# Attention and expert kernel: the last group's second residual sum ahead of the next batch's second low weights

## The chip, the cores and the metric

The kernel runs on one core of a Trainium2 chip. The core has five engines with an instruction queue each: TensorE (matmul), VectorE, ScalarE, GpSimd and SyncE, the last issuing most DMA transfers. They run side by side and wait for each other by semaphores that the kernel names itself. The metric is the device time of one execution in microseconds (us), the median of several runs.

## The reference

Four sequences of 2048 tokens, 256 features each, pass a causal attention without softmax (signs of the inputs as queries and keys, a sigmoid as weights), a residual sum and a layer norm, and then a layer of 32 experts with one expert per token, a residual sum and a second layer norm. Cut to what matters:

```python
Q = ste_sign(x * bq); K = ste_sign(x * bk); V = x * bv     # bq, bk, bv: signs of the biases
scores = jnp.einsum('btd,bsd->bts', Q, K) * scale
attn = jnp.where(causal, jax.nn.sigmoid(scores * 4.0), 0.0)
x = _layernorm(x + jnp.einsum('bts,bsd->btd', attn, V))
# experts: logits = xt @ w_router; top-1 expert, at most C tokens each
y = jnp.einsum('ecf,efh->ech', jax.nn.silu(g) * u, w_down)
x = _layernorm(x + out_tok * gate)
```

## The kernel before

**Tiling.** The attention takes up the first 300 us or so. Each batch (sequence) is cut into four groups of 512 queries. Group g meets 4g + 4 key tiles of 128, one per step, which gives NS = 40 steps per batch: steps 0 to 3 for group 0, 4 to 11 for group 1, 12 to 23 for group 2 and 24 to 39 for group 3. In the last four steps of a group the key tile lies on the diagonal and the step has 512, 384, 256 and 128 query columns. Group 0 has diagonal steps alone.

**A step on the engines.** TensorE computes the scores of a step into one of SB = 4 PSUM banks (line 910, four steps ahead). ScalarE takes the sigmoid twice: into the high weights, rounded (line 703), and back into PSUM in full (line 705). VectorE subtracts the two, which gives the low weights (`low`, line 1202). TensorE then multiplies high and low weights with high and low values (`values`, lines 932 to 934, three matmuls for each of the step's tiles of 128 queries) and adds up over the steps of the group in two PSUM banks, two tiles of 256 columns in each. The scores of step k + 4 wait for the low weights of step k, whose bank they overwrite.

**The end of a group.** When the first two of the group's four tiles are complete, VectorE adds the input to them (`residual`, line 1209, one 128x512 sum for one bank), and later does the same for the other two. The semaphore `pv_done` counts finished value steps: the first sum of a group waits for the group's last step but two, the second for the last step. The next group's first step overwrites both banks; TensorE's first matmul into each waits for the sum that reads it (`res_ready`). The row statistics follow (lines 1216 and 1224), and GpSimd, ScalarE, TensorE and VectorE turn them into the normalised rows, the router's logits and the places in the experts' buffers, spread over the steps of the next group by tables at the top of the file.

**What sets the order.** Each engine's order is written out by the program: `batch` on VectorE runs over the 40 steps, puts `low(b, k)` first in each, and then whatever the tables place at step k. `SUM[g]` holds the steps of the two sums of group g, `ROWS[g]` that of the first two tiles' statistics, `STATS[g]` that of the others and of the aggregation. A step of 40 or more means step k - 40 of the next batch. So `SUM[3] = (40, 41)` puts the first sum of group 3 behind `low` of the next batch's step 0 and the second behind that of its step 1. After the last batch the two sums are written out separately and don't read the table.

```python
                    for g in range(NG):
                        for i in (0, 2):
                            if k == SUM[g][i // 2]:
                                add_pair(b, g, i)
                            if k + NS == SUM[g][i // 2] and not first:
                                add_pair(b - 1, g, i)
                        if k == ROWS[g]:
                            row_statistics(b * NG + g, 0, g % 2)
                        if k + NS == ROWS[g] and not first:
                            row_statistics((b - 1) * NG + g, 0, g % 2)
```

**The experts.** From about 310 us on, TensorE runs gate, up and down projections expert by expert; the order there is a separate program.

Of the kernel before, what the change touches and what calls it, by code (L numbers as in the profile page):

```python
# [38 lines left out]

SUM = {0: (4, 4), 1: (13, 13), 2: (23, 24), 3: (40, 41)}
ROWS = {0: 5, 1: 13, 2: 24, 3: 41}
STATS = {3: 1, 0: 6, 1: 17, 2: 25}
NORM = {3: (6, 6, 7, 7), 0: (10, 11, 11, 11), 1: (21, 22, 23, 23), 2: (30, 31, 31, 32)}
# [18 lines left out]
def bass_postln_attn_moe_kernel(nc, x, bv_q, bv_k, bv_v, w_router, w_gate, w_up, w_down, out):  # L64
# [25 lines left out]
    with ExitStack() as ctx:  # L90
# [1069 lines left out]
        def _(dve):  # L1160
# [150 lines left out]
            def add_pair(b, g, i):  # L1311
                residual(b * NG + g, i, b * NS + END[g] - GT + i + 2, g % 2)

            def batch(b, first, last):
                for k in range(NS):
# [9 lines left out]
# [6 lines that stand above are left out]
# [200 lines left out]
```

How the kernel before makes its waits and increments, by code:

```python
        def atleast(eng, s, value, settle=False):  # L265
            if isinstance(value, int) and value <= 0:
                return
            if settle and not isinstance(value, int):
                value = eng.to_reg(value)
                eng.wait_ge(consts, 11)
            eng.wait_ge(s, value)
# [49 lines left out]
        @block.sync  # L324
# [5 lines left out]
            for h, landed in enumerate((x_half, x_in[0])):
                src = x[0, h * GQ // 2:(h + 1) * GQ // 2, :].rearrange("(i p) d -> p i d", p=P)
                sp.dma_start(xall[:, h * GT // 2:(h + 1) * GT // 2, :], src).then_inc(landed, 16)
            sp.dma_start(bv_row[:, :], bv_v.partition_broadcast(P)).then_inc(bv_row_in, 16)
            load_x(0, 1)
            sp.dma_start(w_r[:, :, :], w_router.rearrange("(c p) e -> p c e", p=P)).then_inc(w_r_in, 16)
            for q in range(2, NG):
                load_x(0, q)
            sp.wait_ge(zero_step, 3)
            zrows = buf_rows.rearrange("(n p r) w -> n p (r w)", p=P, r=ZR)
            for n in range(SLOTS // (P * ZR)):
                sp.dma_start(zrows[n], zero).then_inc(zero_out, 16)
# [6 lines left out]
            def turn_signs(b, q):  # L350
                sp.wait_ge(sgn_ready, b * NG + q + 1)
                sp.wait_ge(scores_ready, (b - 1) * NS + min(NS, OFF[3] + GT * q + GT))
                sp.dma_start(q_t[:, q, :, :].rearrange("p c (i t) -> p (c i) t", t=P),
                             sgn[:, :, :, :].rearrange("p c i d -> p (c i d)"), transpose=True).then_inc(qt_in, 16)
```

## Time and profile before

| | us |
|---|---|
| median of 3 runs | 536.95 |
| lowest, highest | 536.78, 537.89 |
| the profiled execution | 540.78 |
| its span, first to last instruction | 539.1 |
| TensorE matmuls busy | 516.2 (96%) |
| TensorE weight loads busy | 457.1 (85%) |
| VectorE busy | 407.4 (76%) |
| ScalarE busy | 378.9 (70%) |
| GpSimd busy | 377.6 (70%) |

A profile is one execution; the row times below belong to it and not to the median. PE is TensorE (PEld its weight loads), DVE VectorE, ACT ScalarE, POOL GpSimd. Matmuls overlap in the records, since they are pipelined and their ends are modelled: how fast TensorE goes is read from start to start. A timeline row has the start, the duration, the engine, the line, the operation, the output and inputs, their shapes and, in brackets, how long the engine was idle ahead of it and who released it.

### The profile page before, as it was taken

To read this page: it belongs to the slowest core of one execution; us is meant where nothing else is said; L and a number is where in the kernel's file an instruction comes from. 1 tells how busy PE (TensorE), PEld (TensorE's weight loads), DVE (VectorE), ACT (ScalarE), POOL (GpSimd) and SP (SyncE) were. 2 spreads that over 40 slices of the span, in tenths; PEclk is the share of its full clock that TensorE was granted. 3 is DMA by queue.
4 is the path that set the end of the run, shared out by engine and by line. 5 is a ranking of instruction groups with operands and counts; after the bars stand their busy time and mean duration, and the time that the engine had idled before them with its cause. 6 is when DMAs were issued, how large, how long until landed. Compare 5 with 4: busy or idle time off the path is not lost.

```text
span 539.1 us, 12188 instructions
## 1 busy us (share of the span) xinstructions
PE 516.2 (96%) x4021; PEld 457.1 (85%) x4021; DVE 407.4 (76%) x1031; ACT 378.9 (70%) x774; POOL 377.6 (70%) x497
## 2 busy tenths in 40 slices
PE   6999999999999999999999988999999999999992
PEld 5889898898888898988989747999988999999981
DVE  4884877876878948688766636888888888888873
ACT  5886968868878879688786513677767667777752
POOL 4647867776879688777775270577777777787776
PEclk9999999999999999999999999999999999999997
DMA  7995332263332433338741016477586666776211
GB/s 253 374 356 181 87 99 61 79 177 101 109 84 80 124 108 79 91 49 274 229 171 62 2 44 157 125 232 216 179 257 195 198 198 208 220 234 191 76 41 51
DMA packets 91919, 81.54 MB, mean 151 GB/s; under 512 B 31642, under 2 KB 83082, under 8 KB 91856
## 3 DMA queue, kind: packets, MB, share of 16 engines
q1 hardware_dynamic: 84320, 66.38, 41.7%
q0 software_dynamic: 6912, 14.30, 7.7%
q8 instruction: 33, 0.54, 0.4%
q14 instruction: 30, 0.25, 0.2%
q10 hardware_dynamic: 624, 0.07, 0.1%
HBM read 44.33 MB, written 37.90 MB: 153 GB/s over the span
## 4 chain that ended last, share of the span: by engine, by line
PE 86%; DVE 3%; issue 3%; POOL 3%; DMA 2%; ACT 1%; SPq 0%; ACTq 0%; DVEq 0%; POOLq 0%
PE ps L932 11%; PE ps L934 11%; PE ps L933 11%; PE ps L910 10%; PE ps L1096 8%; PE ps L1104 7%; PE ps L1097 7%; PE ps L1122 5%; PE ps L1130 3%; PE ps L1069 3%; PE ps L951 2%; PE ps L964 2%; PE ps L1119 1%; PE ps L1121 1%; PE ps L1120 1%
## 5 line engine op out<-in xcount | busy, mean ns | idle before, releaser
L932 PE MATMUL ps<-v_hl,hl_ring 128*128 128x256 f32 x544 | 178.2, 328 | 1.6 <-DVE xs L1209 1.4
L933 PE MATMUL ps<-v_hl,hl_ring 128*128 128x256 f32 x544 | 153.3, 282 | 0.0
L934 PE MATMUL ps<-v_hl,hl_ring 128*128 128x256 f32 x544 | 153.1, 281 | 0.0
L932 PEld LDWEIGHTS ps<-v_hl,hl_ring 128*128 128x128 f32 x544 | 103.3, 190 | 17.6 <-DVE xs L1209 2.1
L1202 DVE TENSOR_TENSOR hl_ring<-ps,hl_ring 128x512 fp32r<-128x512 f32 (+3 forms) x160 | 94.1, 602 | 21.3 <-ACT ps L705 14.9
L933 PEld LDWEIGHTS ps<-v_hl,hl_ring 128*128 128x128 f32 x544 | 103.4, 190 | 2.7
L703 ACT ACTIVATE hl_ring<-ps 128x512 fp32r<-128x512 f32 (+3 forms) x160 | 86.2, 539 | 24.3 <-PE ps L910 24.0
L934 PEld LDWEIGHTS ps<-v_hl,hl_ring 128*128 128x128 f32 x544 | 103.1, 190 | 0.0
L705 ACT ACTIVATE ps<-ps 128x512 f32<-128x512 f32 (+3 forms) x160 | 87.4, 547 | 0.0
L910 PE MATMUL ps<-q_t,k_t 128*128 128x512 bf16 (+3 forms) x320 | 85.0, 349 | 0.2 <-DVE hl_ring L1202 0.2
L542 POOL DMA_INDIRECT expert_rows<-xrow,slot x64 | 64.4, 1007 | 29.4 <-issue 23.2
L1096 PE MATMUL ps<-hl_ring,v_hl 128*128 128x320 f32 x256 | 80.8, 328 | 0.3 <-DVE hl_ring L1473 0.3
L1097 PE MATMUL ps<-hl_ring,v_hl 128*128 128x320 f32 x256 | 76.0, 309 | 0.0
L626 POOL DMA_INDIRECT out_dram<-alone,ids x55 | 61.5, 1118 | 19.5 <-issue 17.4
L826 ACT ACTIVATE a_buf<-ps 128x320 f32<-128x320 f32 x64 | 27.9, 437 | 43.1 <-PE ps L1104 24.2
L1096 PEld LDWEIGHTS ps<-hl_ring,v_hl 128*128 128x128 f32 x256 | 48.1, 188 | 7.0 <-issue 6.5
L1308 DVE TENSOR_TENSOR v_hl<-xall,v_hl 128x1280 fp32r<-128x1280 f32 x32 | 47.9, 1498 | 7.1 <-issue 7.1
L1097 PEld LDWEIGHTS ps<-hl_ring,v_hl 128*128 128x128 f32 x256 | 48.1, 188 | 0.4
L1104 PE MATMUL ps<-hl_ring,v_hl 128*128 128x320 f32 x256 | 47.9, 309 | 0.0
L495 POOL TENSOR_TENSOR v_hl<-z,v_hl 128x1024 fp32r<-128x1024 f32 x15 | 36.0, 2398 | 12.0 <-ACT v_hl L695 12.0
L741 ACT ACTIVATE v_hl<-xall 128x1280 fp32r<-128x1280 f32 x32 | 40.5, 1264 | 0.2 <-PE ps L934 0.2
L1104 PEld LDWEIGHTS ps<-hl_ring,v_hl 128*128 128x128 f32 x256 | 40.2, 188 | 0.0
(170 smaller groups left out, 1104.4 us busy)
## 6 DMA issues: line engine op xcount, KB each, us to landing
expert_rows<-xs SPq DMA_DIRECT2D x40, 258.0 KB, 5.8
xs<-expert_rows SPq DMA_DIRECT2D x32, 258.0 KB, 2.8
out_dram<-alone SPq DMA_DIRECT2D x16, 512.0 KB
xall<-in_L_ffn_w_gate_dram SPq DMA_DIRECT2D x32, 256.0 KB
xall<-in_L_ffn_w_up_dram SPq DMA_DIRECT2D x32, 256.0 KB
xall<-in_L_ffn_w_down_dram SPq DMA_DIRECT2D x32, 256.0 KB
xall<-in_L_attn_x_dram SPq DMA_DIRECT2D x15, 512.0 KB, 5.6
xs<-expert_rows SPq DMA_DIRECT2D x31, 64.5 KB, 3.4
```

Of the source, the lines that this page charges most:

```text
L542: g_.indirect_dma_start(out=buf_rows, out_offset=bass.IndirectOffsetOnAxis(ap=slot[:, par, i:i + 1], axis=0), in_=xrow[:, par, i, :], in_o ...
L626: g_.indirect_dma_start(out=out_rows, out_offset=bass.IndirectOffsetOnAxis(ap=ids[:, e % NIDS, t:t + 1], axis=0), in_=o_s[e % 3][:, t, :], ...
L703: s_.activation(hl_ring[:, 0, k % WRING, lo:GQ], ps[:, k % SB, lo:GQ], ACT.Sigmoid, scale=0.25)\
L705: s_.activation(ps[:, k % SB, lo:GQ], ps[:, k % SB, lo:GQ], ACT.Sigmoid, scale=0.25)\
L910: last = mm(o, k_t[:, c, j * P:(j + 1) * P], q_t[:, g, c, lo:GQ], start=(c == 0 and not diag), stop=(c == DC - 1), skip_group_check=diag)
L932: mm(o, ah, v_hl[:, 0, j, :], start=(j == 0 and i % 2 == 0), stop=False, skip_group_check=True)
L933: mm(o, ah, v_hl[:, 1, j, :], start=False, stop=False, skip_group_check=True)
L934: last = mm(o, al, v_hl[:, 0, j, :], start=False, stop=(j == GT * g + i), skip_group_check=True)
L1096: mm(o, wh, xh[:, c, :], start=(c == 0), stop=False)
L1097: mm(o, wl, xh[:, c, :], start=False, stop=False)
L1104: last = mm(o, wh, xl[:, c, :], start=False, stop=(c == DC - 1))
L1202: v_.tensor_tensor(hl_ring[:, 1, r, lo:GQ], ps[:, k % SB, lo:GQ], hl_ring[:, 0, r, lo:GQ].bitcast(F32), ALU.subtract).then_inc(al_ready, 1)
```

## The change

One number of a table: the second residual sum of group 3 is placed at step 40, with the first, instead of step 41.

```diff
-SUM = {0: (4, 4), 1: (13, 13), 2: (23, 24), 3: (40, 41)}
+SUM = {0: (4, 4), 1: (13, 13), 2: (23, 24), 3: (40, 40)}
 ROWS = {0: 5, 1: 13, 2: 24, 3: 41}
 STATS = {3: 1, 0: 6, 1: 17, 2: 25}
```

The rows below are VectorE's at the first change of batch; the same stands at the second and third. Row 1202 with 512 columns is `low` of the new batch's step 0, with 384 that of step 1, with 256 and 128 those of steps 2 and 3; rows 1209 are the two sums of the old batch's group 3 (the tile `xs` is the second of the two buffers for sums), and 1191 are keys. Before:

```order
L1202 TENSOR_TENSOR hl_ring<-ps,hl_ring 128x512 [waits pv_done,a_ready,ah_ready]
L1209 TENSOR_TENSOR xs<-ps,xall 128x512 [waits x1_ready,pv_done]
L1202 TENSOR_TENSOR hl_ring<-ps,hl_ring 128x384 [waits pv_done,a_ready,ah_ready]
L1209 TENSOR_TENSOR xs<-ps,xall 128x512 [waits x1_ready,pv_done]
L1216 BN_STATS stats<-xs 128x6 [waits res_ready]
L1216 BN_STATS stats<-xs 128x6
L1216 BN_STATS stats<-xs 128x6 [waits res_ready]
L1216 BN_STATS stats<-xs 128x6
L1224 BN_AGGR mv<-stats 128x2 [waits rstd_step,stats_step]
L1224 BN_AGGR mv<-stats 128x2 x3
L1191 TENSOR_SCALAR k_t<-q_t,qk_sgn 128x512 [waits qt_in]
L1202 TENSOR_TENSOR hl_ring<-ps,hl_ring 128x256 [waits pv_done,a_ready,ah_ready]
```

And with the change:

```order
L1202 TENSOR_TENSOR hl_ring<-ps,hl_ring 128x512 [waits pv_done,a_ready,ah_ready]
L1209 TENSOR_TENSOR xs<-ps,xall 128x512 [waits x1_ready,pv_done] x2
L1202 TENSOR_TENSOR hl_ring<-ps,hl_ring 128x384 [waits pv_done,a_ready,ah_ready]
L1216 BN_STATS stats<-xs 128x6 [waits res_ready]
L1216 BN_STATS stats<-xs 128x6
```

The second sum has changed places with step 1's low weights; the statistics, the keys and all later rows keep their order.

On TensorE nothing moves. The piece of its order at the same place shows who waits for these rows: step 0's value matmuls (12 of them, in two halves of six), and the scores of step 5 behind them.

```order
L932 MATMUL ps<-v_hl,hl_ring 128x256 [waits al_ready,res_ready,ah_ready,v_ready]
L933 MATMUL ps<-v_hl,hl_ring 128x256
L934 MATMUL ps<-v_hl,hl_ring 128x256
L932 MATMUL ps<-v_hl,hl_ring 128x256
L933 MATMUL ps<-v_hl,hl_ring 128x256
L934 MATMUL ps<-v_hl,hl_ring 128x256
L932 MATMUL ps<-v_hl,hl_ring 128x256 [waits res_ready]
L933 MATMUL ps<-v_hl,hl_ring 128x256
L934 MATMUL ps<-v_hl,hl_ring 128x256
L932 MATMUL ps<-v_hl,hl_ring 128x256
L933 MATMUL ps<-v_hl,hl_ring 128x256
L934 MATMUL ps<-v_hl,hl_ring 128x256
```

This is the same before and with the change: the first `res_ready` is the first sum's, the second the second's, and the next row, the scores of step 5, waits for `al_ready`, which low weights of step 1 post.

## Rows read from the trace of the kernel before

**Rows 1.** The page: TensorE's busy time, and the chain that ended last, by engine
```profile
PE 516.2 (96%) x4021; PEld 457.1 (85%) x4021; DVE 407.4 (76%) x1031; ACT 378.9 (70%) x774; POOL 377.6 (70%) x497
...
PE 86%; DVE 3%; issue 3%; POOL 3%; DMA 2%; ACT 1%; SPq 0%; ACTq 0%; DVEq 0%; POOLq 0%
```

**Rows 2.** Who waited for whom, TensorE, 0 to 305 us: total us, times, longest us
```profile
PE ps L932 <- DVE xs L1209: 1.4, 3, 0.6
```

**Rows 3.** Timeline of TensorE at the first change of batch
```profile
83.16 0.28 PE L934 MATMUL ps<-v_hl,hl_ring 128*128 128x256 f32 x1
...
83.94 0.36 PE L932 MATMUL ps<-v_hl,hl_ring 128*128 128x256 f32 x1
...
84.61 0.28 PE L934 MATMUL ps<-v_hl,hl_ring 128*128 128x256 f32 x1
...
85.44 0.39 PE L932 MATMUL ps<-v_hl,hl_ring 128*128 128x256 f32 x1 [0.56 <-DVE xs L1209]
...
86.26 0.61 PE L910 MATMUL ps<-q_t,k_t 128*128 128x512 bf16 x2
...
87.78 0.60 PE L910 MATMUL ps<-q_t,k_t 128*128 128x512 bf16 x2
```

**Rows 4.** Timeline of VectorE at the same place
```profile
83.11 0.68 DVE L1209 TENSOR_TENSOR xs<-ps,xall 128x512 f32<-128x512 f32 x1
84.23 0.56 DVE L1202 TENSOR_TENSOR hl_ring<-ps,hl_ring 128x384 fp32r<-128x384 f32 x1 [0.44 <-issue]
84.70 0.68 DVE L1209 TENSOR_TENSOR xs<-ps,xall 128x512 f32<-128x512 f32 x1
85.30 1.40 DVE L1216 BATCH_NORM_STATS2 stats<-xs 128x6 f32<-128x256 f32 x4
...
87.27 0.62 DVE L1202 TENSOR_TENSOR hl_ring<-ps,hl_ring 128x256 fp32r<-128x256 f32 x2
```

**Rows 5.** Timeline of ScalarE there: the second sigmoid of step 1
```profile
83.65 0.49 ACT L705 ACTIVATE ps<-ps 128x384 f32<-128x384 f32 x1
```

**Rows 6.** Timeline, end of group 0: its last matmul, and the sum behind it
```profile
89.61 0.28 PE L934 MATMUL ps<-v_hl,hl_ring 128*128 128x256 f32 x1
...
89.98 0.69 DVE L1209 TENSOR_TENSOR res<-ps,xall 128x512 f32<-128x512 f32 x1 [0.64 <-issue]
```

**Rows 7.** Timelines of TensorE and VectorE at the third change of batch
```profile
230.60 0.28 PE L934 MATMUL ps<-v_hl,hl_ring 128*128 128x256 f32 x1
...
231.68 0.56 DVE L1202 TENSOR_TENSOR hl_ring<-ps,hl_ring 128x384 fp32r<-128x384 f32 x1 [0.44 <-ACT hl_ring L703]
...
232.06 0.28 PE L934 MATMUL ps<-v_hl,hl_ring 128*128 128x256 f32 x1
...
232.89 0.39 PE L932 MATMUL ps<-v_hl,hl_ring 128*128 128x256 f32 x1 [0.55 <-DVE xs L1209]
```

**Rows 8.** Timelines of VectorE and TensorE at the second change of batch
```profile
157.36 0.56 DVE L1202 TENSOR_TENSOR hl_ring<-ps,hl_ring 128x384 fp32r<-128x384 f32 x1 [0.44 <-ACT hl_ring L703]
158.30 0.69 DVE L1209 TENSOR_TENSOR xs<-ps,xall 128x512 f32<-128x512 f32 x1 [0.39 <-PE ps L934]
158.91 1.40 DVE L1216 BATCH_NORM_STATS2 stats<-xs 128x6 f32<-128x256 f32 x4
...
160.87 0.62 DVE L1202 TENSOR_TENSOR hl_ring<-ps,hl_ring 128x256 fp32r<-128x256 f32 x2
...
157.28 0.28 PE L934 MATMUL ps<-v_hl,hl_ring 128*128 128x256 f32 x1
...
158.44 0.28 PE L934 MATMUL ps<-v_hl,hl_ring 128*128 128x256 f32 x1
...
159.05 0.39 PE L932 MATMUL ps<-v_hl,hl_ring 128*128 128x256 f32 x1 [0.33 <-DVE xs L1209]
...
161.38 0.61 PE L910 MATMUL ps<-q_t,k_t 128*128 128x512 bf16 x2
```

**Rows 9.** Timeline of ScalarE behind the first change of batch: step 5's first sigmoid
```profile
87.29 0.60 ACT L703 ACTIVATE hl_ring<-ps 128x512 fp32r<-128x512 f32 x1 [1.21 <-PE ps L910]
```

## The prediction

> **What bounds the kernel now.** I read the busy shares and the chain of waits first. TensorE's matmuls are busy 96% of the span and carry 86% of the chain that ended last [rows 1]. So an edit on VectorE changes the time only where TensorE waits for it. The view of who waited for whom, cut to the attention (0 to 305 us), names one such wait on the moved line: TensorE stood three times for the residual sums of line 1209, 1.4 us in all, 0.6 us the longest [rows 2]. Three is the number of batch boundaries, and the changed table entry acts at those alone; the last batch ends in code of its own. I then read the timeline at each boundary.
>
> I call the two halves of step 0's value matmuls pair 1 and pair 2 (six matmuls each). Pair 1 needs the first residual sum, pair 2 the second, since each overwrites the PSUM bank that the sum reads. "Low n" is VectorE's line 1202 of step n of the new batch, and "step 39" the last step of the old one.
>
> At the first boundary, pair 1 runs from 83.94 to 84.61, five spacings in 0.67 us, so 0.13 us apart. The next matmul, which opens pair 2, starts only at 85.44 [rows 3]. Of these 0.83 us, 0.70 us is a hole. VectorE shows why: its first sum starts at 83.11, then it is idle 0.44 us ahead of low 1 (84.23), then the second sum starts at 84.70 and takes 0.68 us, to 85.38. Pair 2 follows 0.06 us behind that end [rows 4]. Low 1 waited for ScalarE's second sigmoid of step 1, 83.65 plus 0.49 = 84.14 [rows 5]. So the second sum waits, by its place in the queue, for a ScalarE result that it does not use. Its own input was there: the last matmul of step 39 starts at 83.16 [rows 3], and elsewhere a sum starts 0.37 us behind such a start (89.61 to 89.98) [rows 6], which would be 83.53 here.
>
> The third boundary has the same shape: 232.06 to 232.89, again a hole of 0.70 us, with step 39's last matmul at 230.60 and low 1 at 231.68 [rows 7]. The second boundary differs. Low 1 starts at 157.36, and the second sum at 158.30, behind 0.39 us of idle put down to TensorE; that is 1.02 us behind the start of step 39's last matmul (157.28). The hole is 158.44 to 159.05, so 0.61 - 0.13 = 0.48 us [rows 8].
>
> **The change, part by part.** Nothing is added or removed: in each of three boundaries one 128x512 sum (0.68 us) goes ahead of one 128x384 low weights (0.56 us). The steps are the same on TensorE, ScalarE, GpSimd and SyncE, and no DMA moves.
>
> First boundary. From the start of a sum to that of the next instruction 0.60 us pass (84.70 to 85.30), from low 1 to the next 0.47 us (84.23 to 84.70) [rows 4]. The second sum then starts at 83.11 + 0.60 = 83.71, which is behind the 83.53 above, and ends at 84.39. Pair 2 is due at 84.61 + 0.13 = 84.74 and no longer waits: 0.70 us gained there. Low 1 starts at 83.71 + 0.60 = 84.31, 0.08 us later than now, and ends at 84.87. Who needs it? The scores of step 5, now at 86.26, then at 85.56 [rows 3]: covered by 0.7 us. What is late next is low 2. The row statistics start at 84.31 + 0.47 = 84.78 instead of 85.30, so everything behind them on VectorE is 0.52 us earlier, and low 2 starts at 86.75 instead of 87.27. The scores of step 6 need it. They start 0.51 us behind low 2's start at all three boundaries (87.78 behind 87.27, 161.38 behind 160.87 [rows 3, 4, 8]). Their place behind the matmuls ahead of them would be 87.78 - 0.70 = 87.08; VectorE allows 86.75 + 0.51 = 87.26, or 0.06 us less if those 0.51 us hold some slack. So 0.52 to 0.58 us of the 0.70 us stay. I take **0.55 us** for the first boundary, and by the same rows **0.55 us** for the third.
>
> The spacing decides here, so a rule of the Trainium skill is weighed against it. The row shows the instruction behind the sum starting at 85.30, 0.08 us before the sum's end at 85.38 [rows 4]. The Trainium skill (VectorE: DVE Perf Modes, The DRAIN you can't avoid) says that the next operation does not start until the pipeline is empty. By a strict end-to-start chain the second sum would start at 83.79, low 1 at 84.47 and the statistics at 85.03, and each boundary would keep 0.27 us. The rows measure the overlap, so I go by 0.60 us.
>
> Second boundary. Here the second sum already starts when TensorE's signal comes, 158.30, and it cannot start sooner by standing earlier. If the signal is as late as in this trace, pair 2 stays at 159.05, and low 1, whose inputs were ready at 157.36, is now queued behind the waiting sum: 158.30 + 0.60 = 158.90. The statistics start at 159.37 instead of 158.91, low 2 at 161.33, the scores of step 6 at 161.78 to 161.84 instead of 161.38: a loss of 0.40 to 0.46 us. If the signal comes 0.37 us behind the matmul's start, as in rows 6, the sum runs 157.65 to 158.33, pair 2 is due at 158.57, low 1 starts at 158.25, the statistics at 158.72, low 2 at 160.68 and the scores of step 6 at 161.13 to 161.19: a gain of 0.19 to 0.25 us. I take a loss of **0.2 us**, between these ends and nearer to the one that this trace shows.
>
> Behind the boundaries I cost nothing: at the first ScalarE idles 1.21 us for the scores of step 5 before it takes up step 5 at 87.29 [rows 9], so it moves up with TensorE, and the statistics, which GpSimd waits for, come earlier by 0.52 us at two boundaries. What a boundary gives is a shift of all that follows.
>
> Sum: -0.55 - 0.55 + 0.2 = **-0.9 us**, between -0.65 (late signal at the second) and -1.4 (prompt one, top of each span). The profiled execution took 540.78 us with a span of 539.1; the median of the runs is 536.95 (536.78 to 537.89). I put the difference on the median: 536.0 us. Differences under 0.2%, about 1.07 us, are what a measurement of this kernel cannot tell from none, so the forecast lies inside that band and near its edge.
>
> **Rivals.**
>
> *All three boundaries gain (535.3 us).* If TensorE, 0.55 us earlier through the second batch, meets the second boundary as it met the others, that boundary gives 0.55 us too: -1.65 us. For: two of three show this form, and the late signal occurs once. Against: at the second boundary TensorE was not stopped ahead of pair 1, and the sum had to wait for it even behind low 1.
>
> *The gain is absorbed (about 537.0 us).* ScalarE and VectorE share later due points with TensorE in the new batch (normalising, transposes, routing), and if one of those is set by ScalarE's own work, TensorE waits there for what it gained. For: ScalarE has little idle time between steps 6 and 9. Against: the wait of 1.21 us in rows 9, which shows ScalarE behind TensorE and not ahead of it.
>
> *A new wait in front of low weights (slower, 538.3 us).* The second sum now stands between low 0 and low 1, and everything behind it waits for step 39's last matmul. In the first boundary, with the sum starting at s, low 2 starts at s + 0.60 + 0.47 + 1.97 (85.30 to 87.27) and the scores of step 6 0.51 us later; this equals 87.78 at s = 84.23, 1.07 us behind that matmul's start. Beyond that point each 0.1 us costs 0.1 us. The second boundary, at 1.02 us, already loses 0.40 to 0.46 us, since low 1 had been done early there. If the signal came 1.5 us behind the matmul at the other two, all three would lose 0.45 us, 1.35 us in all: 538.3 us. Against: no row shows 1.5 us, and the release of rows 6 is 0.37 us. The Trainium skill (Perfetto Trace Analysis, Tensor Engine Instruction) says that a matmul's reported end is computed, and that its semaphore goes out only when PSUM has acknowledged the writes. By that rule the shown ends don't bound the signal; the 1.02 us of rows 8 agree with it.
>
> That the change does something else than it says is excluded: three pairs of VectorE steps change places.
>
> **How the numbers follow.** Forecast (two gain, the second between its ends): 0.48. All three gain: 0.25. Absorbed: 0.13. New wait: 0.14. Faster by over 0.2%: all of the second case and about a quarter of the first (-1.07 to -1.4), 0.37. Slower by over 0.2%: most of the last, 0.12. The rest, 0.51, lies within. The range: below, all three gain plus the scatter of the runs (the lowest is 0.17 below the median) and some for phases that shift, 534.9; above, the absorbed case and the half of the new wait, 537.7.
>
> **What would show it.** Right: second sums at the first and third boundary start 0.6 us behind the first ones; the wait of TensorE on line 1209 falls from 1.4 to near 0.4 us or less; low 2 is 0.5 us nearer to step 39 there; a short wait appears at the scores of step 6. The idle time of VectorE at line 1209 put down to TensorE at the second boundary grows. Wrong: TensorE still waits 0.5 us ahead of pair 2, or sums that start over 1 us behind step 39's last matmul at two or more boundaries, or the gain seen at 90 us but gone before 150 us.

## The result, and the profile after

The change made the kernel slower: 538.35 us (median of 19 runs) against 537.08 us for the kernel before (19 runs beside them), a ratio of 1.0022 with a 95% interval of 1.0014 to 1.0029. That is 1.27 us, just over the 0.2% that a measurement of this kernel can tell. The forecast was 0.9 us the other way, and 538.35 lies outside its range.

The execution profiled before took 540.78 us while the kernel's runs lie at 537, so the span of the changed kernel's profile (536.4 us) must not be held against that trace's 539.1.

The page of the changed kernel, the lines that answer to [rows 1]:

```profile
PE 512.6 (96%) x3983; PEld 457.6 (85%) x4021; DVE 407.6 (76%) x1031; ACT 380.7 (71%) x774; POOL 384.7 (72%) x497
...
PE 88%; DVE 4%; issue 3%; POOL 2%; DMA 2%; ACT 0%; SPq 0%; ACTq 0%; DVEq 0%; POOLq 0%
```

The record of the changed kernel lacks 38 matmuls (3983 against 4021), so its busy time of TensorE says nothing beside [rows 1]. Who waited for whom on TensorE, 0 to 305 us (total us, times, longest):

```profile
PE ps L970 <- ACT lg_t L725: 1.2, 3, 0.4
PE ps L910 <- DVE hl_ring L1202: 1.0, 4, 0.3
```

The wait on line 1209 [rows 2] is gone, and a wait of the scores (L910) on the low weights (L1202) has come at the changes of batch. Whether the first was ever there in an ordinary execution of the kernel before is the first thing to ask.

The third change of batch in the changed kernel, VectorE and then TensorE, which answers to [rows 7]:

```profile
228.49 0.69 DVE L1209 TENSOR_TENSOR xs<-ps,xall 128x512 f32<-128x512 f32 x1
...
230.08 0.69 DVE L1209 TENSOR_TENSOR xs<-ps,xall 128x512 f32<-128x512 f32 x1 [0.90 <-PE ps L934]
...
230.69 0.55 DVE L1202 TENSOR_TENSOR hl_ring<-ps,hl_ring 128x384 fp32r<-128x384 f32 x1
...
233.11 0.62 DVE L1202 TENSOR_TENSOR hl_ring<-ps,hl_ring 128x256 fp32r<-128x256 f32 x2
...
229.70 0.28 PE L934 MATMUL ps<-v_hl,hl_ring 128*128 128x256 f32 x1
...
231.57 0.28 PE L934 MATMUL ps<-v_hl,hl_ring 128*128 128x256 f32 x1
...
233.09 0.28 PE L934 MATMUL ps<-v_hl,hl_ring 128*128 128x256 f32 x1
...
233.59 0.60 PE L910 MATMUL ps<-q_t,k_t 128*128 128x512 bf16 x2 [0.22 <-DVE hl_ring L1202]
...
234.62 0.28 PE L934 MATMUL ps<-v_hl,hl_ring 128*128 128x256 f32 x1
```

The last value matmuls (L934) of four steps stand here: step 39 of the old batch at 229.70, steps 0, 1 and 2 of the new one at 231.57, 233.09 and 234.62. VectorE starts the first sum 1.21 us *ahead* of step 39's last matmul (228.49 against 229.70). It then idles 0.90 us and starts the second sum 0.38 us behind that matmul. Low 1, low weights of step 1, stands behind it, and low 2 starts at 233.11. TensorE had no hole in step 0's values (231.57 is 1.87 us behind 229.70), but step 1's last value matmul starts at 233.09 and the scores of step 6 only at 233.59: 0.50 us where 0.12 is usual (232.16 to 232.28 in the kernel before, shown further down), so 0.38 us lost.

### The profile page after: what moved, and what is told of

Same layout as the page of the kernel before. It is cut to its first block, busy times and chain, and to the rows that moved or that the text cites. A ratio compares the mean times of both kernels' runs of the same rounds, so it can differ in the third digit from the quotient of the medians.

```text
span 536.4 us, 12150 instructions
## 1 busy us (share of the span) xinstructions
PE 512.6 (96%) x3983; PEld 457.6 (85%) x4021; DVE 407.6 (76%) x1031; ACT 380.7 (71%) x774; POOL 384.7 (72%) x497
## 4 chain that ended last, share of the span: by engine, by line
PE 88%; DVE 4%; issue 3%; POOL 2%; DMA 2%; ACT 0%; SPq 0%; ACTq 0%; DVEq 0%; POOLq 0%
PE ps L932 12%; PE ps L933 11%; PE ps L934 11%; PE ps L910 10%; PE ps L1096 8%; PE ps L1104 7%; PE ps L1097 7%; PE ps L1122 5%; PE ps L1130 3%; PE ps L1069 3%; PE ps L951 2%; PE ps L964 2%; PE ps L1119 1%; PE ps L1121 1%; PE ps L1120 1%
## 5 line engine op out<-in xcount | busy, mean ns | idle before, releaser
L934 PE MATMUL ps<-v_hl,hl_ring 128*128 128x256 f32 x544 | 153.1, 281 | 0.0
L1202 DVE TENSOR_TENSOR hl_ring<-ps,hl_ring 128x512 fp32r<-128x512 f32 (+3 forms) x160 | 93.9, 601 | 19.1 <-ACT ps L705 13.6
L934 PEld LDWEIGHTS ps<-v_hl,hl_ring 128*128 128x128 f32 x544 | 103.1, 190 | 0.0
L910 PE MATMUL ps<-q_t,k_t 128*128 128x512 bf16 (+3 forms) x286 | 77.4, 345 | 3.8 <-issue 1.3
L626 POOL DMA_INDIRECT out_dram<-alone,ids x55 | 57.0, 1035 | 16.6 <-issue 14.4
L1096 PEld LDWEIGHTS ps<-hl_ring,v_hl 128*128 128x128 f32 x256 | 48.1, 188 | 7.0 <-issue 6.5
L1097 PEld LDWEIGHTS ps<-hl_ring,v_hl 128*128 128x128 f32 x256 | 48.2, 188 | 0.4
L844 ACT ACTIVATE alone<-z,zrs 128x256 f32<-128x256 f32 x54 | 29.0, 594 | 17.6 <-POOL zrs L613 16.3
```

The lines of the kernel that those rows point to most:

```text
L626: g_.indirect_dma_start(out=out_rows, out_offset=bass.IndirectOffsetOnAxis(ap=ids[:, e % NIDS, t:t + 1], axis=0), in_=o_s[e % 3][:, t, :], ...
L910: last = mm(o, k_t[:, c, j * P:(j + 1) * P], q_t[:, g, c, lo:GQ], start=(c == 0 and not diag), stop=(c == DC - 1), skip_group_check=diag)
L934: last = mm(o, al, v_hl[:, 0, j, :], start=False, stop=(j == GT * g + i), skip_group_check=True)
L1096: mm(o, wh, xh[:, c, :], start=(c == 0), stop=False)
L1097: mm(o, wl, xh[:, c, :], start=False, stop=False)
L1202: v_.tensor_tensor(hl_ring[:, 1, r, lo:GQ], ps[:, k % SB, lo:GQ], hl_ring[:, 0, r, lo:GQ].bitcast(F32), ALU.subtract).then_inc(al_ready, 1)
```

## The experiments

Two theories went in. Theory 1: at the changes of batch VectorE is usually ahead of TensorE, so the moved sum finds its input missing and holds low weights 1 and all behind them. Theory 2: the boundaries are as in the first profile, and the time is lost later. After the first four runs, theory 1 took its later form: executions come in two kinds, and the change's sign follows from the kind. In the *late* kind (the kernel before near 540.5 us) VectorE and ScalarE start over 1 us behind the matmul that they wait for, at certain places; in the *prompt* kind (near 537 us) 0.3 to 0.4 us behind it.

### The kernel before again, in runs at 540.5 us

No edit.

> The kernel before once more, for its profile. Theory 1 (the profile read for the prediction was not the usual execution; usually VectorE is ahead of TensorE at every change of batch, so that the second sum waits for step 39 even behind the low weights of step 1): the span is about 535.4 us, and at all three changes of batch the second sum starts about 0.4 us behind step 39's last matmul, with idle time before it, and TensorE's wait on line 1209 is under 0.3 us in all. Theory 2 (the boundaries are as in the first profile, and what they give is lost later): holes of 0.7 us ahead of pair 2 at the first and third change of batch again.

The kernel before had a median of 540.54 us in these runs, 3.5 us more than beside the changed kernel, and its span was 539.0. All three changes of batch have the form of [rows 3]; TensorE's waits in the attention:

```profile
PE ps L932 <- DVE xs L1209: 1.7, 3, 0.6
```

The expected span of 535.4 us and the missing holes did not come, so by this profile alone theory 2 holds. But the time had moved too: the first profile and this one are of executions near 540.5 us, and the result is of executions near 537.

### The wait alone, low weights 1 behind step 39

```diff
-                atleast(dve, pv_done, n - WRING + 1)
+                atleast(dve, pv_done, b * NS if k == 1 else n - WRING + 1)
```

> The order of before, but low weights of step 1 of a new batch wait for the last value step of the old batch. Theory 1 (low weights 1, and all behind them, held by that wait are the cost): as slow as the change, 1.002 to 1.003, about +1.2 us, and a wait of 0.3 to 0.4 us at the scores of step 6. Theory 2 (the cost comes from where the second sum stands or from what the statistics set off later): less than half of that, 1.000 to 1.001.

1.0002 (0.9991 to 1.0013), beside the same runs of the kernel before: theory 1, as it stood then, had 1.002 to 1.003 here and missed. Where the kernel before takes 540.5 us, low weights 1 come behind that signal anyway (84.30, released by ScalarE, 1.06 us behind step 39's last matmul at 83.24), and the wait costs nothing.

### The first pair's statistics directly behind the first sum

```diff
-ROWS = {0: 5, 1: 13, 2: 24, 3: 41}
+ROWS = {0: 5, 1: 13, 2: 24, 3: 40}
```

> The order of before, but the first pair's statistics go from behind the second sum to directly behind the first sum (0.7 us of VectorE work into its idle time). Theory 1: low weights of step 2 come 0.3 to 0.7 us earlier at each change of batch; if they hold the scores of step 6 in the kernel before, 0.998 to 0.999, if they don't, 1.000. Theory 2: no change, or slower if the low weights of step 1 are held.

1.0018 (1.0007 to 1.0029), slower, where theory 1 expected 1.000 or less and theory 2 allowed for a loss. At the first change of batch the timeline shows the first sum at 83.34 and the second at 85.19, 1.85 us apart instead of 1.59 (83.11 to 84.70 in [rows 4]): in these runs low weights 1 and the second sum set TensorE's hole, and the 0.75 us of statistics don't fit into 0.44 us of idle time.

### The change at the first change of batch alone

```diff
-                            if k + NS == SUM[g][i // 2] and not first:
+                            if k + NS == (40 if g == 3 and b in BOUND else SUM[g][i // 2]) and not first:
```

with `BOUND = (1,)` and the table of before.

> The change at the first change of batch alone. Theory 1 (each change of batch costs 0.4 us): +0.4 us, 1.0005 to 1.0012. Theory 2 (a loss that grows out of one place, or a gain there): outside of that, either about 0 or the whole +1.2 us.

0.9987 (0.9974 to 1.0000): by the median a *gain* of about 0.7 us, with none at the edge of the interval. Theory 1, as it stood, had a loss. The traces are sharper than the times. From step 39's last value matmul to step 2's last, the first change of batch took 5.62 us in the kernel before of this set (the first two rows) and 5.06 us here (the last two): 0.56 us gained, as the prediction had it for such a boundary (0.55). The second and third change of batch, left as before, took 5.66 and 5.65 us here.

```profile
83.66 0.28 PE L934 MATMUL ps<-v_hl,hl_ring 128*128 128x256 f32 x1
...
89.28 0.28 PE L934 MATMUL ps<-v_hl,hl_ring 128*128 128x256 f32 x1
...
83.41 0.28 PE L934 MATMUL ps<-v_hl,hl_ring 128*128 128x256 f32 x1
...
88.47 0.28 PE L934 MATMUL ps<-v_hl,hl_ring 128*128 128x256 f32 x1
```

### The change and the kernel before again

In the next set of runs the kernel before took 537.34 us, so this is the prompt kind.

> The change as it is, beside the kernel before on one chip. Theory 1 now: executions come in two kinds. In one (kernel before near 540.5 us) TensorE's signals are late at about 19 places, VectorE is late at the changes of batch and the change gains 0.4 to 0.55 us at each, so the ratio is 0.996 to 0.998. In the other (kernel before near 537 us) the signals are prompt, VectorE is ahead, the second sum waits for step 39 and holds low weights 1, and the ratio is 1.002. Theory 2 (the change costs the same 1.2 us whatever the kind): 1.002 on either.

1.0016 (1.0007 to 1.0024), about 0.9 us slower: the result again.

> The kernel before, for its profile in the kind of execution that this chip gives. Near 537 us: theory 1 expects the logits' maximum (line 1233) 0.3 us behind line 970 near 71 us, the second sum at the first change of batch 1 us or more ahead of pair 2's due time and no hole ahead of pair 2. Near 540.5 us: holes of 0.7 us as in the first profile.

This is the profile that the prediction should have had. The span is 535.2 us. Third change of batch, VectorE and then TensorE:

```profile
227.56 0.69 DVE L1209 TENSOR_TENSOR xs<-ps,xall 128x512 f32<-128x512 f32 x1
...
228.65 0.56 DVE L1202 TENSOR_TENSOR hl_ring<-ps,hl_ring 128x384 fp32r<-128x384 f32 x1 [0.40 <-ACT ps L705]
...
229.15 0.69 DVE L1209 TENSOR_TENSOR xs<-ps,xall 128x512 f32<-128x512 f32 x1
...
231.72 0.42 DVE L1202 TENSOR_TENSOR hl_ring<-ps,hl_ring 128x256 fp32r<-128x256 f32 x1
...
228.78 0.28 PE L934 MATMUL ps<-v_hl,hl_ring 128*128 128x256 f32 x1
...
230.65 0.28 PE L934 MATMUL ps<-v_hl,hl_ring 128*128 128x256 f32 x1
...
232.16 0.28 PE L934 MATMUL ps<-v_hl,hl_ring 128*128 128x256 f32 x1
232.28 0.60 PE L910 MATMUL ps<-q_t,k_t 128*128 128x512 bf16 x2
...
233.32 0.28 PE L934 MATMUL ps<-v_hl,hl_ring 128*128 128x256 f32 x1
```

Low 1 still waits for ScalarE (0.40 us), and the second sum follows low 1 without idle time, 0.37 us behind step 39's last matmul; the idle time ahead of it that theory 1 had expected is not there. But all of this comes before pair 2 is due. There is no hole to fill: from step 39's last matmul to step 0's last 1.87 us pass (228.78 to 230.65), as in the changed kernel (229.70 to 231.57). Low 1 starts 0.13 us *before* step 39's last matmul here and 0.99 us behind it with the change; low 2 stands 2.94 us behind it here and 3.41 us with the change, 0.47 us later. And from step 1's last value matmul to step 2's last 1.16 us pass here (232.16 to 233.32) and 1.53 us with the change (233.09 to 234.62). 0.37 us at each of three changes of batch is 1.1 us of the 1.27 us measured. The whole stretch, from step 39's last value matmul to step 2's last, says the same at all three: 4.54 us each here, 4.91, 4.92 and 4.92 us with the change.

### What the sum's place and the lateness of low weights 2 cost

Four kernels in one more set of runs, the kernel before at 537.48 us. First the wait alone again.

> The order of before, with low weights 1 waiting for the old batch's last value step, in the kind of execution that this chip gives. Theory 1, prompt kind (kernel before near 537 us): low weights 1 come 0.5 us later than in the kernel before, low weights 2 too, and the scores of step 6 wait 0.3 to 0.4 us at each change of batch: 1.001 to 1.003, as slow as the change. Late kind (near 540.5 us): ScalarE's sigmoid comes after that signal anyway, 1.000. Theory 2 (the place of the sum costs, not the wait): 1.000 in both kinds.

1.0020 (1.0005 to 1.0035): without moving the sum, the wait costs about what the change costs. The expectation had the size right and the place wrong. Here the sum, queued behind low 1, is late too, and TensorE stands ahead of pair 2 (84.40 to 84.87 at the first change of batch, 0.47 us where 0.12 is usual); the scores of step 6 then come late enough by themselves. So this run shows that a wait at that place costs, but not that the lateness of low 2 does; the next two show that.

```profile
PE ps L932 <- DVE xs L1209: 0.6, 3, 0.2
```

Then the change with the first pair's statistics in VectorE's idle time, between the two sums:

```diff
                             if k + NS == SUM[g][i // 2] and not first:
                                 add_pair(b - 1, g, i)
+                                if i == 0:
+                                    row_statistics((b - 1) * NG + g, 0, g % 2)
                         if k == ROWS[g]:
                             row_statistics(b * NG + g, 0, g % 2)
-                        if k + NS == ROWS[g] and not first:
-                            row_statistics((b - 1) * NG + g, 0, g % 2)
```

> The change, with the first pair's statistics (0.7 us) moved from behind low weights 1 to between the two sums, where VectorE idles 0.9 us in the prompt kind. Theory 1, prompt kind: the second sum still starts 0.37 us behind step 39's last matmul, but low weights 2 come 0.6 to 0.7 us earlier than with the change, the wait at the scores of step 6 is gone, and the loss with it: 1.000 (0.9993 to 1.0005). Late kind: 0.996 to 0.999. Theory 2 (the lateness of low weights 2 is not what costs): 1.002 in the prompt kind.

0.9990 (0.9980 to 1.0001). The sums stand as in the change, the second again 0.37 us behind step 39's last matmul (228.21); only low 2 is earlier. Third change of batch:

```profile
226.99 0.69 DVE L1209 TENSOR_TENSOR xs<-ps,xall 128x512 f32<-128x512 f32 x1
...
228.58 0.69 DVE L1209 TENSOR_TENSOR xs<-ps,xall 128x512 f32<-128x512 f32 x1
...
230.96 0.61 DVE L1202 TENSOR_TENSOR hl_ring<-ps,hl_ring 128x256 fp32r<-128x256 f32 x2
...
231.59 0.28 PE L934 MATMUL ps<-v_hl,hl_ring 128*128 128x256 f32 x1
...
232.75 0.28 PE L934 MATMUL ps<-v_hl,hl_ring 128*128 128x256 f32 x1
```

Low 2 starts 0.63 us ahead of step 1's last value matmul, where the change had it 0.02 us behind, and step 2 follows in 1.16 us again. The whole stretch takes 4.54 us at all three changes of batch, as in the kernel before. The loss is gone with the lateness of low 2. And all of the statistics behind low 2:

```diff
-ROWS = {0: 5, 1: 13, 2: 24, 3: 41}
-STATS = {3: 1, 0: 6, 1: 17, 2: 25}
+ROWS = {0: 5, 1: 13, 2: 24, 3: 42}
+STATS = {3: 2, 0: 6, 1: 17, 2: 25}
```

on top of the change.

> The change, with all of group 3's statistics one step later, behind low weights 2. Theory 1, prompt kind: low weights 2 come 1.8 us earlier, no wait at the scores of step 6; the norm's rows come some 0.6 us later, which ScalarE may feel at step 6: between 0.999 and 1.0005, clearly under the change's 1.002. Theory 2: 1.002 or more.

1.0004 (0.9995 to 1.0013): the loss is gone here too, and the trace has 4.54 us at each change of batch. And the change at the first change of batch alone, in the same set of runs:

> The change at the first change of batch alone. Theory 1: in the prompt kind a third of the loss, 1.0003 to 1.001; in the late kind a gain of 0.4 to 0.6 us, 0.9985 to 0.9995.

1.0004 (0.9995 to 1.0013), about 0.2 us. By size a third of the loss (0.4 us) is within its interval, but so is none. The trace decides: 4.92 us at the changed place (83.51 to 88.43), 4.54 us at the other two.

### The change and its repair once more

> The change once more beside the kernel before. Theory 1: if this chip gives the late kind (kernel before near 540.5 us), the holes ahead of pair 2 are there to be filled and the ratio is 0.996 to 0.998; in the prompt kind (near 537 us) 1.002 as twice before. A ratio of 1.000 or more in the late kind would mean that only part of the prediction's gain exists even there.

1.0022 (1.0013 to 1.0032), with the kernel before at 537.21 us. The late kind did not come.

> The change with the first pair's statistics between the two sums. Theory 1: in the late kind 0.996 to 0.999; in the prompt kind 0.999 again. Rival: its 0.999 was the chip's noise, 1.000 here in the prompt kind.

1.0002 (0.9993 to 1.0010). So the repair takes the change's loss away, twice; that it beats the kernel before is not shown.

### Making VectorE late on purpose

What made the first profile's VectorE late? These are the matmul that turns the logits (L970) and VectorE's maximum of them (L1233), in that trace, in three successive batches:

```profile
70.86 0.27 PE L970 MATMUL ps<-ident,lg_t 128*128 128x128 f32 x1
...
72.36 0.29 DVE L1233 TENSOR_REDUCE top<-ps 128x4 f32<-128x128 f32 x1 [2.31 <-PE ps L970]
...
145.30 0.29 DVE L1233 TENSOR_REDUCE top<-ps 128x4 f32<-128x128 f32 x1 [0.78 <-PE ps L970]
...
219.83 0.29 DVE L1233 TENSOR_REDUCE top<-ps 128x4 f32<-128x128 f32 x1 [2.31 <-PE ps L970]
```

and in the kernel before at 535.2 us:

```profile
71.04 0.27 PE L970 MATMUL ps<-ident,lg_t 128*128 128x128 f32 x1
...
71.35 0.29 DVE L1233 TENSOR_REDUCE top<-ps 128x4 f32<-128x128 f32 x1 [1.11 <-PE ps L970]
```

VectorE starts 1.50 us behind the matmul in the one and 0.31 us in the other. In the first trace the waits of 2.31 us stand ahead of the first and the third change of batch, those with the larger holes, and the wait of 0.78 us ahead of the second, where VectorE was early. From there the lateness runs on: in the first trace GpSimd's values for the next batch start at 77.96, released by VectorE, ScalarE's rounding of them (L695) at 80.38, and behind it in ScalarE's queue the new batch's first weights at 81.35; in the trace at 535.2 us these are 76.94, 79.37 and 80.33, each 1.0 us earlier. To set the lateness by hand, the maximum in the first three batches first waited for step 32's value matmuls.

```diff
-                    dve.wait_ge(logits_done, G + 1)
+                    dve.wait_ge(logits_done, G + 1); atleast(dve, pv_done, G // NG * NS + 33 if G in (2, 6, 10) else 0)
```

> The kernel before, with VectorE's maximum of group 2's logits (line 1233, step 33) in the first three batches made to wait for the value matmuls of step 32, which holds VectorE there some 1 to 2 us, as the late signal did in the first profile. Theory 1: GpSimd's values, ScalarE and VectorE then reach the changes of batch later, TensorE waits there for the sums, and the kernel is 1 to 3 us slower than before: 1.002 to 1.006. The first sum starts within 0.3 us of step 39's last matmul, and a hole of 0.4 to 0.8 us stands ahead of pair 2.

1.0237 (1.0223 to 1.0251), 12 us: far too strong. VectorE stood idle 3.08 us ahead of the maximum, where it was 1.11 us, and TensorE then waited 6.4 us in all for low weights before the batch was over, 2.1 us at the longest (77.63 the first).

> The change, with the same hold. Theory 1: the sign turns over: 0.8 to 1.6 us faster than late_before, as the prediction worked it out for the first profile, where the change without the hold is 1.2 us slower than before. Theory 2 (the change costs 1.2 us whatever VectorE's state): 1.2 us slower than late_before. Rival 3 (the gain ahead of pair 2 is absorbed): the same as late_before.

1.0223 (1.0210 to 1.0237). The change is no loss here, but the intervals overlap and the state is not that of the first profile: nothing is settled by this pair. So the lateness was set by 0.95 us of work in place of a wait, on a tile `scrap` that nobody reads:

```diff
-                    dve.wait_ge(logits_done, G + 1)
+                    dve.wait_ge(logits_done, G + 1); [v_.reciprocal(scrap[:, G // NG, :, :], iota_d[:, :, :]) for _ in range(G in (2, 6, 10))]
```

> The kernel before, with one reciprocal more (about 0.94 us of VectorE work on a tile that nobody reads) ahead of line 1233 at step 33 in the first three batches: about as late as line 1233 stood in the first profile (72.36 against 71.35 us), and without the longer stop of the hold. Theory 1: line 1275 and GpSimd's values come 0.9 us later, the first sum starts within 0.2 us of step 39's last matmul, and a hole of about 0.7 us stands ahead of pair 2 at each change of batch: 1.5 to 3.5 us slower than before, 1.003 to 1.0065.

1.0042 (1.0027 to 1.0057). The hole ahead of pair 2 is back at all three changes of batch, 0.62 us each; the first profile had 0.70, 0.48 and 0.70. The first sum stands 0.43 us ahead of step 39's last matmul (83.39), not within 0.2 us of it as expected, and the shorter wait ahead of pair 1 that the late kind has is not back. So this is two thirds of the late kind: 5.25, 5.27 and 5.27 us from step 39's last value matmul to step 2's last, against 4.54 us in the prompt kind and 5.62, 5.65 and 5.70 us in the profile at 540.5 us. The first change of batch:

```profile
71.41 0.95 DVE L1232 RECIPROCAL scrap<-iota_d 128x128 f32<-128x128 f32 x1 [1.12 <-PE ps L970]
72.27 0.23 DVE L1233 TENSOR_REDUCE top<-ps 128x4 f32<-128x128 f32 x1
...
82.96 0.68 DVE L1209 TENSOR_TENSOR xs<-ps,xall 128x512 f32<-128x512 f32 x1
...
84.55 0.28 PE L934 MATMUL ps<-v_hl,hl_ring 128*128 128x256 f32 x1
...
85.29 0.39 PE L932 MATMUL ps<-v_hl,hl_ring 128*128 128x256 f32 x1 [0.46 <-DVE xs L1209]
```

> The change, with the same reciprocal. Theory 1: 0.55 us faster than busy_before at each of three changes of batch, 1.65 us in all, so a ratio to the kernel before that is 0.003 under busy_before's. Theory 2 (the change costs 1.2 us whatever VectorE's state): 0.002 above it. Rival 3 (the gain ahead of pair 2 is absorbed): the same.

1.0015 (1.0006 to 1.0024), beside 1.0042: with VectorE late, the change *gains* 0.27%, 1.45 us (1.08 us by the medians, 539.20 and 538.12), where it loses 1.2 us without the reciprocal. In its timeline the two sums follow each other (83.03, 1.50 us for both) and pair 2 starts without a wait, 84.61 to 84.74:

```profile
83.03 1.50 DVE L1209 TENSOR_TENSOR xs<-ps,xall 128x512 f32<-128x512 f32 x2
...
84.61 0.28 PE L934 MATMUL ps<-v_hl,hl_ring 128*128 128x256 f32 x1
84.74 0.28 PE L932 MATMUL ps<-v_hl,hl_ring 128*128 128x256 f32 x1
...
87.34 0.61 PE L910 MATMUL ps<-q_t,k_t 128*128 128x512 bf16 x2 [0.22 <-DVE hl_ring L1202]
```

The last row is the other half of it: the second sum still waits for step 39 (it starts at 83.83, 0.37 us behind the matmul at 83.46), and the scores of step 6 still lose 0.38 us. From step 39's last value matmul to step 2's last the changed kernel takes 4.92, 4.92 and 4.91 us, just what it takes without the reciprocal. So the changed kernel takes the same time there in both states. What differs is the kernel before: it takes 4.54 us there when VectorE is early and 5.26 us with the reciprocal, and the change looks like a loss of 0.38 us beside the one and like a gain of 0.34 us beside the other.

## Why the prediction was wrong

**What bounds the kernel: the failed step.** "The third boundary has the same shape ... The second boundary differs" took two holes of 0.70 us as the kernel's own and the second boundary as the exception. None of the three holes exists in a prompt execution, the kind that the result is of. There low 1 starts 0.05 to 0.13 us ahead of step 39's last matmul at every boundary (the second boundary of the first profile, 0.08 us behind it, comes nearest), the second sum 0.37 to 0.43 us behind that matmul, and pair 2 does not wait. So the prediction's sum started from a kernel before that is 1.1 us too long at two boundaries (5.65 and 5.66 us against 4.54) and 0.6 us at the other (5.13). For the changed kernel its working was right: it put the scores of step 6 3.85 to 3.91 us behind step 39's last matmul for a prompt signal at the second boundary (161.13 to 161.19 against 157.28), and 3.89 us were measured (233.59 against 229.70). But it set them against 4.10 us (161.38), where the kernel before has 3.50 us (232.28 against 228.78).

Two signs were there and not used. The profiled execution stood 3.8 us above the median, 540.78 against 536.95, and the text put "the difference on the median", that is, it assumed that the place it costed at -0.55 us twice exists in the runs at 536.95. And in the trace, though not in the rows taken from it, the wait of line 1233 was 2.31 us ahead of two boundaries and 0.78 us ahead of the third; the text asked what VectorE waited for at the boundary and did not ask what had made it late.

**First and third boundary, -0.55 us each.** Right for the state that it describes: 0.56 us by the traces at the one such boundary that was run in the late kind (0.7 us by the times, interval 0 to 1.4 us), and 1.08 to 1.45 us over three boundaries with VectorE late by 0.95 us of extra work (0.34 us each by the traces, since that makes the kernel before less late). In the prompt runs, which the forecast was for, the term is +0.37 us each.

**Second boundary, +0.40 to +0.46 us with a late signal.** This was the right mechanism with nearly the right price: low 1 queued behind the waiting sum, low 2 0.47 us later, the scores of step 6 held. It measured 0.37 us. But it needs no late signal: at 230.08 the sum starts 0.38 us behind the matmul, the usual release of [rows 6], and the loss is there all the same. The text gave 0.19 to 0.25 us of *gain* for that case, since it compared with the first profile's kernel before, whose second sum had itself been held to 158.30, with a hole of 0.48 us behind it.

**Rivals.** "A new wait in front of low weights" named mechanism and place, with 0.45 us at each of three boundaries; its chance of 0.14 was too small because its condition was set by rows of the late state (a signal 1.5 us behind the matmul). What decides is not how late the signal is but how early VectorE is in the kernel before. A signal as late as the rival asked for was seen once, in the run with the statistics directly behind the first sum: at its second change of batch the second sum starts 1.76 us behind step 39's last matmul (159.40 against 157.64). "All three boundaries gain" has been seen with the reciprocal alone. "Absorbed" was not seen: with the reciprocal a gain of 1.08 to 1.45 us was left in the whole time.

**VectorE's spacing.** The 0.60 us from a sum's start to the next one held: 230.08 to 230.69 is 0.61 us, 0.08 us short of the sum's 0.69 us. The strict end-to-start chain that the prediction weighed is again not what the rows show; the sum would not have come out right by it either. The prediction took it from one sentence of the Trainium skill (VectorE: DVE Perf Modes, The DRAIN you can't avoid); the same paragraph adds that a next operation that is not held starts earlier, and with that the 0.08 us of overlap agree.

**What stays open.** Why VectorE and ScalarE start over 1 us behind TensorE's matmuls at some places of the program, in some sets of runs, is not known. It does not go with one chip: the runs at 540.54 us and a later set at 537.60 us of the same kernel have the same chip number in the record. The Trainium skill (Perfetto Trace Analysis, Tensor Engine Instruction) allows for it, since a matmul's semaphore goes out only when PSUM has acknowledged its writes and the reported end is computed; no run here shows what holds it. That this lateness makes the whole of the late kind is argued from the traces; 0.95 us of work by hand brought two thirds of it. The change itself was not run in such a set, only one third of it, and the whole of it with the lateness set by hand.

## What to carry to other kernels

Before costing an edit, compare the profiled execution's time with the median of the runs: where they differ by more than the edit is worth (here 3.8 us against 0.9), look for the place that the profile alone has, and treat places of the same role that look unlike as two states of one place. A forecast is a difference: the changed kernel can be worked out to 0.05 us and the sign still be wrong, if the kernel before is taken from an unusual execution. An in-order engine's wait is cheap or dear by what is queued behind it: a result that is needed soon should not stand behind an operation whose input another engine still owes, and where it must, the idle time should be given work that is due anyway (here 0.7 us of statistics took the whole loss of 0.2% away). To learn the sign of an edit in a state that the chip shows only now and then, set the state by hand, with a small piece of work and not with a wait.

## What the runs showed of the hardware that was not expected

The same program had medians of 537.1 to 537.6 us in six sets of runs and 540.54 us in one (29 runs, 539.18 to 541.84), with granted clocks of 0.992 to 0.995 in the slower set and 0.989 to 0.995 in the others. Nearly all of the difference lies at the three changes of batch: start for start, TensorE falls back there by 0.36 us ahead of pair 1 and 0.71 us ahead of pair 2 each time, 3.2 us in all, between the profiles at 535.2 and 539.0 us. In the slower set VectorE's maximum started 1.50 us behind the matmul that it waits for, where 0.31 us is usual (71.36 to 72.85, and in the first profile 70.86 to 72.36), although TensorE's own matmuls went on at their 0.12 us. ScalarE shows it too, so it is not VectorE's alone: one first sigmoid starts 2.45 us behind the start of its scores in the slower set's profile, and 0.64 us behind it at the same place in the profile at 535.2 us.

```profile
188.06 0.59 PE L910 MATMUL ps<-q_t,k_t 128*128 128x512 bf16 x2
...
190.51 0.60 ACT L703 ACTIVATE hl_ring<-ps 128x512 fp32r<-128x512 f32 x1 [2.66 <-PE ps L910]
```

And 0.95 us more of VectorE work at one step of each of three batches cost 2.3 us in the end (1.0042), nearly all of it at the changes of batch ten microseconds later (0.72 us at each).
